# A two-batch cross-attention and FFN kernel on Trainium2: another order of three engines' work in its first stage

## What is computed

```python
def fake_quant(x, scale, zp):
    q = jnp.clip(jnp.round(x / s + z), 0.0, 255.0)
    return (q - z) * s
def xattn(x1, x2, ...):                  # x1 (2,1024,2048), x2 (2,2048,2048)
    return jnp.matmul(fake_quant(x1, ...), fake_quant(x2, ...))
...
x = x + xattn(layernorm(x), ctx_4096, ...)
x = x + ffn(layernorm(x), W_base, b_base, W_router, lora_A, lora_B)
```

## Time and profile before

| what | value |
|---|---|
| time, median of 3 runs | 1034.18 us (1033.33 to 1034.25) |
| the profiled execution | 1034.23 us, of which span 1032.5 us |
| PE busy | 970.2 us (94%) |
| VectorE busy | 798.8 us (77%) |
| ScalarE busy | 470.5 us (46%) |
| chain that ended last | PE 77%, VectorE 8%, ScalarE 8%, issue 4%, DMA 3% |
| first stage's chunk matmuls | x1536, the first at 37.3, the last at 309.4 us |

### The profile page before, as it was taken

The page is one execution under the profiler, slowest core; times in us unless marked ns, Lnnn a source line. Parts: engine busy times, 40 slices in busy tenths (PEclk is TensorE's granted clock), DMA queues, the critical chain, the costliest instruction groups (busy, mean ns, idle before and its releaser), DMA issues.

```text
span 1032.5 us, 15016 instructions
## 1 busy us (share of the span) xinstructions
PE 970.2 (94%) x5847; PEld 524.6 (51%) x5847; DVE 798.8 (77%) x1503; ACT 470.5 (46%) x492; POOL 18.7 (2%) x40
## 2 busy tenths in 40 slices
PE   0487999899999999999999999999999999999997
PEld 0355666566669944444444444444444444444443
DVE  6767888688762788996788687775798798798785
ACT  4769889687753335543355343212223322322310
POOL 0000000000000000000000000000000000000000
PEclk9889999899999999999999999999999999999999
DMA  7837686568734335876575576228743242232220
GB/s 303 328 126 286 241 286 227 184 246 323 267 143 134 124 113 175 257 246 212 171 235 153 180 248 208 67 78 290 243 148 112 77 146 104 87 134 89 95 72 30
DMA packets 62590, 185.64 MB, mean 180 GB/s; under 512 B 7432, under 2 KB 19768, under 8 KB 56248
## 3 DMA queue, kind: packets, MB, share of 16 engines
q1 hardware_dynamic: 58360, 174.18, 47.9%
q10 hardware_dynamic: 2880, 8.39, 2.1%
q0 software_dynamic: 1280, 2.12, 2.1%
HBM read 151.07 MB, written 33.60 MB: 179 GB/s over the span
## 4 chain that ended last, share of the span: by engine, by line
PE 77%; DVE 8%; ACT 8%; issue 4%; DMA 3%; ACTq 0%; DVEq 0%
PE pair L1628 32%; PE pair L1651 28%; PE pair L1492 11%; PE pair L1607 4%; DVE stats L847 3%; ACT ctx_u L655 2%; ACT xt L661 2%; DMA w_r<-in_w_n 1%; ACT q1u L638 1%; PE pair L1597 1%; DVE xt L919 1%; ACT pair L677 1%; ACT q1T L646 1%; ACT x2p L669 1%; DVE acc L938 1%
## 5 line engine op out<-in xcount | busy, mean ns | idle before, releaser
L1628 PE MATMUL pair<-x2p,w_p 128*128 128x512 f16 x1536 | 336.7, 379 | 0.0
L1628 PEld LDWEIGHTS pair<-x2p,w_p 128*128 128x128 f16 x1536 | 150.2, 98 | 180.7 <-DVE w_p L1114 0.3
L1492 PE MATMUL pair<-q1T,ctx_q 128*128 128x342 f16 x1536 | 235.3, 315 | 0.0
L1492 PEld LDWEIGHTS pair<-q1T,ctx_q 128*128 128x128 f16 x1536 | 150.5, 99 | 77.5
L1651 PE MATMUL pair<-x2p,w_slot 128*128 128x512 f16 x768 | 169.2, 379 | 0.0
L750 ACT ACTIVATE sq<-pair,lsc 128x512 f32<-128x512 f32 x64 | 43.6, 682 | 234.4 <-PE pair L1607 200.7
L1651 PEld LDWEIGHTS pair<-x2p,w_slot 128*128 128x128 f16 x768 | 75.0, 98 | 90.7
L778 ACT ACTIVATE w_slot<-w_q,usc 128x1024 f16<-128x1024 f32 x32 | 36.5, 1146 | 95.2 <-DVE usc L1322 27.2
L1651 PE MATMUL pair<-x2p,x2p 128*128 128x512 f16 x336 | 74.3, 379 | 0.0
L655 ACT ACTIVATE ctx_u<-ctx_f,par 128x2048 uint8<-128x2048 f32 x32 | 66.6, 2082 | 3.0 <-DMA ctx_f<-in_ctx 1.6
L919 DVE SCALAR_TENSOR_TENSOR xt<-pair,par,xt 128x342 f32<-128x342 f32 (+1 forms) x96 | 54.4, 567 | 12.6 <-PE pair L1492 11.2
(11 more groups left out here) (200 smaller groups left out, 1069.6 us busy)
## 6 DMA issues: line engine op xcount, KB each, us to landing
ctx_f<-in_ctx SPq DMA_DIRECT2D x32, 1024.0 KB, 7.2
rows<-in_x SPq DMA_DIRECT2D x16, 1024.0 KB, 8.5
xt<-in_xT SPq DMA_DIRECT2D x32, 512.0 KB, 4.6
w_r<-in_w_n SPq DMA_DIRECT2D x32, 512.0 KB, 6.8
w_f<-in_w_t SPq DMA_DIRECT2D x32, 512.0 KB, 5.6
outT<-u SPq DMA_DIRECT2D x64, 256.0 KB, 3.2
w_q<-in_w_t SPq DMA_DIRECT2D x32, 512.0 KB, 5.4
x_kept<-xt ACTq DMA_DIRECT2D x16, 512.0 KB, 4.8
```

The source lines that it names most:

```text
L1492: ins = M.matmul(bank[at % RING][:, 0:W3], ctx_q[n % NQ][:, k, :], q1T[b][:, k, c * W3:(c + 1) * W3], start=(k == 0), stop=(k == KT - 1))
L1628: M.matmul(base_bank(m)[:, :], w_p[j % 2][wh][:, k, :], x2p[0][:, k, xh, t], start=(k == 0 and q == 0), stop=(k == KT - 1 and q == 2))
```

## The change

Nothing is computed otherwise; the calls stand in another order on SP, ScalarE, VectorE and PE. `LN_AT` is a list of the steps in which row tiles 10 to 15 have their statistics. Row tiles 8 and 9 are made ahead of step 0. The load of the low-rank and router weights (`ar_f`) moves to step 15 on SP.

```diff
+LN_AT = [2, 4, 7, 9, 11, 13]
...
             load_ctx(4)
             load_ctx(5)
-            sp.dma_start(ar_f[:, :, :], ar).then_inc(ar_landed, 16)
+            load_rows(TT + 2)
             for n in range(3, STEPS):
                 load_xt(n)
                 if n + 3 < STEPS:
                     load_ctx(n + 3)
-                if n % 2 and (n + 1) // 2 < TT:
-                    load_rows(TT + (n + 1) // 2)
+                if n in LN_AT:
+                    load_rows(TT + 2 + LN_AT.index(n))
+                if n == JT - 1:
+                    sp.dma_start(ar_f[:, :, :], ar).then_inc(ar_landed, 16)
...
             ln_copy(TT - 1)
+            ln_std_of(TT)
             ctx_bytes_of(3)
-            ln_std_of(TT)
+            ln_bytes_of(TT)
             ln_std_of(TT + 1)
+            ln_bytes_of(TT + 1)
 
             for n in range(STEPS):
-                T = TT + n // 2
-                if n % 2 == 0 and n >= 4 and T < ROWS:
-                    ln_std_of(T)
                 col_add_of(n)
                 hi_of(n)
+                if n in LN_AT:
+                    ln_std_of(TT + 2 + LN_AT.index(n))
                 sq_of(n)
                 if n + 4 < STEPS:
                     ctx_bytes_of(n + 4)
-                if n % 2 == 0 and T < ROWS:
-                    ln_bytes_of(T)
-                if n % 2 and T < ROWS:
-                    ln_copy(T)
+                if n in (0, 1):
+                    ln_copy(TT + n)
+                if n in LN_AT:
+                    ln_bytes_of(TT + 2 + LN_AT.index(n))
+                if n - 1 in LN_AT:
+                    ln_copy(TT + 2 + LN_AT.index(n - 1))
...
             for T in range(2, TT):
                 ln_stats_of(T)
+                if T == 6:
+                    take_y(0, 0)
+                if T == 7:
+                    take_y(1, 0)
+                ln_scale_of(T - 1)
                 if T in (3, 5, 7):
                     ctx_ready_of(T // 2 - 1)
-                if T == 6:
-                    take_y(0, 0)
-                ln_scale_of(T - 1)
-            take_y(1, 0)
             ln_scale_of(TT - 1)
             bound(0)
...
             take_y(0, 1)
             xscale(0)
+            ln_scale_of(TT)
             take_y(2, 0)
             ln_stats_of(TT + 1)
             take_y(1, 1)
-            ln_scale_of(TT)
+            ln_scale_of(TT + 1)
             take_y(2, 1)
             take_y(0, 2)
             ctx_ready_of(3)
             take_y(1, 2)
-            ctx_ready_of(4)
             lo_of(0)
             take_y(2, 2)
             acc_of(0)
+            ctx_ready_of(4)
             lo_of(1)
             acc_of(1)
+            ln_stats_of(TT + 2)
...
                 take_y(n, 0)
-                if n % 2 and T < ROWS:
-                    ln_scale_of(T)
+                if n - 1 in LN_AT:
+                    ln_scale_of(TT + 2 + LN_AT.index(n - 1))
                 lo_of(n - 1)
...
                 acc_of(n - 1)
-                if n % 2 == 0 and T < ROWS:
-                    ln_stats_of(T)
-                if n == JT - 1:
-                    bound(1)
                 if n == JT:
                     take_y(n, 1)
                 else:
                     take_y(n, 2)
+                if n in LN_AT:
+                    ln_stats_of(TT + 2 + LN_AT.index(n))
+                if n == JT - 1:
+                    bound(1)
...
                     chunk(0, 1)
-                    turn_bound(0)
             chunk(2, 0)
+            turn_bound(0)
             chunk(1, 1)
             row_sum(TT - 1)
             chunk(2, 1)
             pe.wait_ge(par_step, 8)
-            for n in range(3):
-                chunk(n, 2)
+            chunk(0, 2)
+            turn(TT)
+            chunk(1, 2)
+            chunk(2, 2)
...
                 chunk(n, 0)
+                chunk(n, 1)
                 if n == 3:
-                    turn(TT)
-                chunk(n, 1)
-                if n % 2 == 0 and m < TT:
-                    turn(TT + m)
-                if n % 2 and m < TT:
-                    row_sum(TT + m)
+                    row_sum(TT)
+                    turn(TT + 1)
...
                 chunk(n, 2)
+                if n - 2 in LN_AT:
+                    T = TT + 2 + LN_AT.index(n - 2)
+                    row_sum(T - 1)
+                    turn(T)
```

More of the change, by code:

```diff
@@ L1529, in _ @@
             pe.wait_ge(par_step, 8)
-            for n in range(3):
-                chunk(n, 2)
+            chunk(0, 2)
+            turn(TT)
+            chunk(1, 2)
+            chunk(2, 2)
             for n in range(3, STEPS):
-                m = (n - 2) // 2
                 if n == JT:
@@ L1547, in _ @@
                     chunk(n, 2)
-                    row_sum(TT + m)
+                    row_sum(ROWS - 1)
                     continue
                 chunk(n, 0)
+                chunk(n, 1)
                 if n == 3:
-                    turn(TT)
-                chunk(n, 1)
-                if n % 2 == 0 and m < TT:
-                    turn(TT + m)
-                if n % 2 and m < TT:
-                    row_sum(TT + m)
+                    row_sum(TT)
+                    turn(TT + 1)
                 if n == JT + 5:
```

## The result

The changed kernel takes **1028.51 us** (median of 4 runs, 1028.0 to 1028.86) against 1034.22 us before (4 runs): a ratio (changed over before) of 0.9946, 95% interval 0.9934 to 0.9958. The forecast was 1028.7. The profiled execution took 1028.86 us, 1027.1 of it span.

The account below looks back on a forecast made before the run. Before the boundary no engine is full, so the order of handoffs between PE, VectorE and ScalarE decides; afterwards PE is full. Reordering starts the boundary's chunks 5.5 us earlier: 1034.23 - 5.5 = 1028.7, range 1024.5 to 1033.0.

Parts of the forecast that it names:

- The front: Up to 64 us: scale(6) waits behind take (1,0), so tile 6's bytes and all behind come 1.6 us later.
- 64 to 104: The 4.25 us copy wait goes, 3.3 before chunk (4,1) comes; step 4's last take ends at 104.2 to 104.3, as before.
- The loop: Batch 1's row tiles: row step 9.3 us plus plain step 5.95 makes a pair 15.3, against 16.12; five pairs 76.4.
- unshortened loop: Rival: ScalarE stays the link, a pair stays at 16.12, 4.1 us comes back, total 1032.8; chance 0.12.
- the gain is this wait: Loop: the gain is VectorE's wait for the high half shrinking from 1.62 to 0.86 us; moving statistics only shifts them.
- PE's slack of 2.2: Between 93.5 us and the boundary PE keeps up, ready at 192.0, with 2.2 us to spare.
- The clock at the boundary: Batch boundary: granted clock stays at 0.50 of 2.4 GHz, so the two chunks there keep their 7.60 us.
- the clock holds: Rival at the batch boundary: two chunks take 4.81 us instead of 7.60, total 1025.9; chance 0.18.
- The other two rivals: Front's worse clock, 1030.6, chance 0.10; slower, buffer waits lowering PE's clock between 93 and 193, e.g. 1036.5, chance 0.10.
- The front's clock: Rival: longer PE idling at the front slows chunk (0,1) and the next, 1.9 us on the chain, 1030.6; chance 0.10.
- Moved transfers: Row tiles are mostly requested some 16 us before use, A and router weights at step 15, five steps ahead: hidden.
- From the chunk after them all as before, shifted: Sign of being right: behind the boundary's chunks everything runs as before, only shifted by the gain, taken as 5.5 us.

Follow-up runs that it names:

- experiment 3: Kernel before, with only the change's VectorE order for batch 0's row tiles (take (1,0) ahead of scale(6), context tiles behind the scales): 1035.86 us, ratio 1.0015.
- experiment 4: Changed kernel with one move undone: at row tile 7, VectorE's take (1,0) stands behind scale(6), the context tile and scale(7) again; 1020.71 us, ratio 0.9873.
- experiment 1: Kernel before, with two moves alone: VectorE's row-tile statistics behind the step's last take, ScalarE's root behind the high half; 1031.08 us, ratio 0.9975.
- experiment 2: Changed kernel with a row tile's statistics ahead of the step's last take again: 1031.55 us, ratio 0.9984.
- experiment 6: Changed kernel with PE's row sum and turn in the loop back between a step's second and third chunk: 1028.24 us, ratio 0.994.
- experiment 7: Changed kernel with take (1,0) behind the scales and PE's boundary sums one chunk later, behind chunk (16,2): 1017.76 us, ratio 0.984.
- second profile: The changed kernel, unaltered, profiled once more without timing rounds: 1028.12 us.

## Why the prediction was right, point by point

- **The front.** Right for the changed kernel: bytes and chunk (2,0) within 0.4, the mechanism as told. Alone it costs 1.6 too (experiment 3), but there the parts are others. What the text did not see is that the delay was avoidable at the price of one line: the scale was ready to run at 46.9, where VectorE then stood idle for 6.70 us until 53.69. The sum holds for the change as made, and the change leaves about 6.5 us there (experiment 4; the rest of its 7.8 is the clock at the boundary and the FFN).
- **64 to 104.** Right in its waits: the one for the copy goes (tile 8's turn came three chunks forward, (1,2), (2,2) and (3,0), where the text and the sentence under the order have two), and the one for take (3,0) comes (3.42). That step 4 ends at 104.27, as forecast, is two errors that cancel: step 3 ends at 98.30, not 98.0, and the plain step behind it takes 5.97, where the text put 6.2, though its own sum for a plain step is 5.95. With the front's order alone (experiment 3) step 4 ended at 106.53, so this stretch made good about 2 us; no run has its moves by themselves.
- **The loop.** Right, and by the named cause: 15.29 a pair; two moves alone give it (experiment 1), without the statistics' move it is 16.26 (experiment 2). That PE's turn takes no part follows from experiment 6. The unshortened loop was a fair rival: it is what comes without the statistics' move.
- **"... the gain is this wait".** This leaves a part out. When VectorE is through step 15 the changed kernel is 3.18 ahead (189.08 and 192.26); 2.0 of the 5.15 at the sums comes only behind that, since the last row tile's copy no longer holds up the boundary (experiment 1). The sum has this in it, because it goes by absolute times; the text doesn't name it.
- **PE's slack of 2.2.** It bears: in experiment 7 PE fell 2.25 behind by its clock and the boundary did not move.
- **The clock at the boundary.** The step "I keep that price" was mis-sized: 6.45 instead of 7.60, 1.15 to the good. The sums, too, took 1.83 instead of the 2.2 that the text carried over; they started 0.43 late, so that 196.46 hits the forecast 196.4 by luck. The rival that the clock holds came true only in other orders.
- **The other two rivals.** The front's clock cost little: chunk (0,1) took 3.66 (3.82 in the second profile), not 3.43, and the rival's 1.9 did not come. Between 93 and 193 the mean clock was 0.98, over the 0.97 that the text set as a sign of being wrong; behind the wait at chunk (4,1) two chunks took 6.48, and PE's slack covered it.
- **Moved transfers.** Right: from 60 to 200 neither VectorE nor ScalarE waits for a landing transfer, and the weights moved to step 15 are asked for at 172.68, land 7.3 us later and are first read at 224.9.
- **"From the chunk after them all as before, shifted".** This failed: 1.3 is lost again at the start of the FFN (0.18 of it at a transpose that waits 0.69 instead of 0.51, 1.12 at the fifth group), since the FFN's own margin against its round trip is near zero: 7.33 before, against the 7.4 from which PE is late. In the second profile 0.24 was lost at that group instead of 1.12.

The clock's 1.15 and the FFN's 1.3 nearly cancel, so that the total is nearer (0.2 us) than its parts: the order was forecast well, the last tenths are luck.

## What to carry to other kernels

Follow each engine's list by hand with starts of consecutive rows: that gave the waits of this stage to a few tenths, through 140 us and a new order. Look in such a list for a short operation that others wait for (a scale of six small operations, 1.21 us) behind one that itself waits (a take of an unfinished chunk): turning the two round was worth 6.5 us in this stage, more than the whole change. And before a gain is carried to the end, look in the stages behind it for chains with a margin near zero, such as a round trip through memory: there a part of it may go again.

## What the hardware did that was not expected

- PE's clock after a wait is not given by the wait's length. Behind a wait of 3.42 us before chunk (4,1) two chunks took 6.48 (changed kernel), 7.67 (experiment 7), or the next chunk ran at full clock, 2.48 (experiment 4, twice), and the work up to there is the same in experiments 4 and 7. At the front, chunk (0,1) took 3.43 in the kernel before and 4.44 in experiment 1, again with the same work up to there. At the boundary waits of 1.27 and 1.28 were followed by 6.45, 6.48, or three times by 4.81. Only without a wait it was the same each time: 2.49 and 2.49 or 2.48, in three profiles of three. The Trainium skill (TensorE: Matmul & The Clock Gate, Part 1) calls the number of slow matmuls at a start "run-variable"; the rows of experiments 4 and 7 show such a difference in mid-kernel too.
- The round trip of a few bytes through memory took from 7.12 to 8.50 us at the same place of the program, 7.61 and 8.50 in two profiles of the same kernel.
